# The last feed-forward stage of a four-layer kernel: order on VectorE, GpSimd and TensorE changed, layer-norm's scaling moved to ScalarE

## The reference, cut to what matters

```python
h = _layernorm(x) * (1 + cb) + sb
x_diff = h[:, None] - select_mean_diff[None, :, None, :]          # 8 experts
x_diff = x_diff / norm(x_diff)
score = (einsum('nds,bntd->bnts', select_weight, x_diff) ** 2).sum(-1)
gate = sigmoid(imp_slope * (score - imp_center))                  # per expert and token
sel_scale, sel_idx = gate.max(axis=1), gate.argmax(axis=1)
debias, bias, upd, dgn = rows of the tables at sel_idx
out = (1 - sel_scale) * h + sel_scale * (bias + dgn @ (upd^T (h - debias)))
x = x + gb * out
```

## Time and profile before

| | before |
|---|---|
| median of three runs | 1896.47 us |
| the profiled execution | 1898.01 us, its span 1895.8 us |
| mean granted clock of PE | 0.95 of full |
| busy share of PE, DVE, ACT, POOL | 88%, 71%, 44%, 53% |
| the chain that ended last | PE 56%, DVE 24%, issue 10% |
| the changed stage | from about 1752 us to the end |

### The profile page before, as it was taken

The page is one execution under the profiler, slowest core; times in us unless marked ns, Lnnn a source line. Parts: engine busy times, 40 slices in busy tenths (PEclk is TensorE's granted clock), DMA queues, the critical chain, the costliest instruction groups (busy, mean ns, idle before and its releaser), DMA issues.

```text
span 1895.8 us, 41681 instructions
## 1 busy us (share of the span) xinstructions
PE 1662.4 (88%) x14144; PEld 1200.9 (63%) x14144; DVE 1344.2 (71%) x3492; ACT 831.1 (44%) x1691; POOL 996.0 (53%) x1089
## 2 busy tenths in 40 slices
PE   5999997899996999999999879999867777999896
PEld 3666664799983555555555547777655555887443
DVE  5899996576654666767676657888745666887786
ACT  5556553222223566565656543333223333443442
POOL 2576676565553456564646354555543223666343
PEclk8999998899997999999999979999999888999988
DMA  7000000100026554546354300000001000000111
GB/s 263 18 18 17 12 18 9 35 12 9 11 48 142 115 104 101 111 88 125 76 122 93 72 7 15 12 8 8 23 27 44 14 14 20 12 14 17 33 45 53
DMA packets 70939, 94.13 MB, mean 50 GB/s; under 512 B 10461, under 2 KB 65165, under 8 KB 67597
## 3 DMA queue, kind: packets, MB, share of 16 engines
q1 hardware_dynamic: 70812, 92.41, 20.6%
HBM read 62.10 MB, written 29.49 MB: 48 GB/s over the span
## 4 chain that ended last, share of the span: by engine, by line
PE 56%; DVE 24%; issue 10%; ACT 5%; POOL 2%; DMA 1%; DVEq 1%; SPq 1%; ACTq 0%; POOLq 0%
PE PS L1173 19%; PE PS L2275 4%; PE PS L2365 3%; DVE negmax L2616 3%; PE PS L1362 3%; PE PS L573 2%; DVE l_acc L1782 2%; DVE st L521 2%; ACT pw L2518 2%; PE PS L2300 2%; PE PS L2220 2%; PE PS L2378 2%; DVE xn L542 1%; PE PS L843 1%; DVE rt_eq L1552 1%
## 5 line engine op out<-in xcount | busy, mean ns | idle before, releaser
L2616 DVE TENSOR_REDUCE negmax<-PS 128x2 f32<-128x512 f32 (+1 forms) x384 | 247.2, 686 | 166.3 <-PE PS L2275 160.6
L604 POOL TENSOR_TENSOR X<-X,y_sb 128x512 f32 (+1 forms) x128 | 163.2, 1275 | 113.7 <-DVE y_sb L599 108.7
L1173 PE MATMUL PS<-we_hi,h_parts 128*128 128x512 f32 x512 | 181.8, 411 | 16.5 <-DVE l_acc L1782 16.4
L2518 ACT ACTIVATE pw<-PS 128x512 f32<-128x512 f32 x256 | 139.2, 600 | 75.5 <-PE PS L2275 75.5
L583 ACT ACTIVATE hT<-PS,modT 128x256 f32<-128x256 f32 x256 | 130.4, 562 | 84.6 <-PE PS L573 83.1
L599 DVE TENSOR_TENSOR y_sb<-PS,ga_sb 128x512 f32<-128x512 f32 x96 | 66.1, 688 | 134.2 <-PE PS L2842 42.6
L1173 PE MATMUL PS<-l_h_parts,lut_hi 128*128 128x256 f32 (+1 forms) x704 | 132.7, 290 | 7.5 <-POOL l_h_parts L1327 7.5
L533 POOL TENSOR_TENSOR rs<-mv,eps 128x2 f32<-128x2 f32 x128 | 29.0, 226 | 187.8 <-DVE mv L526 187.6
L1173 PEld LDWEIGHTS PS<-we_hi,h_parts 128*128 128x128 f32 x512 | 98.2, 192 | 42.7 <-DVE l_acc L1782 15.0
L573 PE MATMUL PS<-ident,xn 128*128 128x128 f32 x512 | 85.3, 292 | 37.9 <-DVE xn L542 29.9
L1173 PEld LDWEIGHTS PS<-l_h_parts,lut_hi 128*128 128x128 f32 (+1 forms) x704 | 110.0, 191 | 10.2 <-issue 5.4
(11 more groups left out here) (328 smaller groups left out, 4585.1 us busy)
## 6 DMA issues: line engine op xcount, KB each, us to landing
ga_sb<-ga_dram SPq DMA_DIRECT2D x128, 128.0 KB, 2.9
qk_dram<-qk_parts SPq DMA_DIRECT2D x64, 192.0 KB, 2.8
KS<-qk_dram SPq DMA_DIRECT2D x32, 384.0 KB, 5.8
QS<-qk_dram SPq DMA_DIRECT2D x32, 384.0 KB, 9.0
qk_dram<-qk_parts SPq DMA_DIRECT2D x64, 128.0 KB, 2.8
wmod<-in_wmod SPq DMA_DIRECT2D x4, 1536.0 KB, 12.8
qk_dram<-qk_parts SPq DMA_DIRECT2D x64, 64.0 KB, 2.4
y_out<-X SPq DMA_DIRECT2D x16, 256.0 KB, 2.2
```

Of the source, the lines that this page charges most:

```text
L604: pool.tensor_tensor(xb(b), xb(b), y_sb[b.par][:, :, :], ALU.add).then_inc(s.x.sem, 1)
L1173: last_ = pe.matmul(out, x.bitcast(F32R), y.bitcast(F32R), start=start and n == 0, stop=stop and n == 2)
L2518: act.activation(to.rearrange("p a n -> p (a n)"), bank(4 + (2 * n + pr) % 3), ACT.Exp).then_inc(s.prob.sem, 1)
L2616: dve.tensor_reduce(to, src, AX.X, ALU.max, negate=True).then_inc(s.max.sem, 1)
```

## The change

In the last stage only:

- DVE no longer normalises batches 1 to 15; ACT does it with `ln_apply_scalar`, placed behind the exponential and ahead of `modulate`. Batch 0 is normalised on DVE by the stage before, as it was.
- POOL computes `shift` for these batches behind `ln_rstd`, and both now stand behind the gated residual.
- DVE's `choice` of i-1 stands directly behind `ratio`, ahead of `y1` of i-2, and the statistics of i+2 are last in the slot.
- PE's `out` of i-2 stands ahead of the transpose of i+1.
- The stage's signals get the two counts of `shift` per batch (`"qs": 2`).

```diff
-                       "tk": 7, ..., "y_ps": 1, "y1": 2},
+                       "tk": 7, ..., "y_ps": 1, "y1": 2, "qs": 2},
...
                 if (i - 1).ok:
                     rows_T(i - 1)
-                ahead(ln_transpose, pe, pl, i, 1)
                 if (i - 2).ok:
                     out(i - 2)
+                ahead(ln_transpose, pe, pl, i, 1)
                 if i.ok:
                     norms(i)
                     tokens(i)
...
                 if (i - 1).ok:
                     route_exp(act, pl, s, i - 1)
+                if (i + 1).ok and i.ok:
+                    ln_apply_scalar(act, pl, s, i + 1)
                 ahead(modulate, act, pl, i, 1)
...
-            def slot(i):
-                ahead(ln_apply, dve, pl, i, 1)
-                ahead(ln_stats, dve, pl, i, 2)
+
+
+            def slot(i):
                 if (i - 2).ok:
...
                 if (i - 1).ok:
                     ratio(i - 1)
+                    choice(i - 1)
                 if (i - 2).ok:
...
-                if (i - 1).ok:
-                    choice(i - 1)
+                ahead(ln_stats, dve, pl, i, 2)
...
             def slot(i):
-                ahead(ln_rstd, pool, pl, i, 2)
                 if (i - 2).ok:
                     gate_on_pool(pool, pl, s, i - 2, l3_y1[:, :, :], s.y1(i - 2))
+                ahead(ln_rstd, pool, pl, i, 2)
+                if i.reg is not None or 1 <= (i + 2).off < B:
+                    ln_shift(pool, pl, s, i + 2, 1)
```

More of the change, by code:

```diff
@@ L263, in build @@
             "L3_ffn": {"p_ps": 1, "hsq": 1, "sq": 1, "mx": 1, "ht": 1, "zr": 3, "z": 1, "zT_ps": 1,
-                       "tk": 7, "ed": 1, "e": 1, "g": 1, "oms": 1, "gT_ps": 1, "s_ps": 1, "zz": 1, "y_ps": 1, "y1": 2},
+                       "tk": 7, "ed": 1, "e": 1, "g": 1, "oms": 1, "gT_ps": 1, "s_ps": 1, "zz": 1, "y_ps": 1, "y1": 2, "qs": 2},
             "L2_attn": {"state_ps": 1, "state": 1},
```

## The result

The changed kernel takes 1906.98 us (median of 6 runs, 1903.03 to 1909.88), the kernel before on the same chip 1896.49 (6 runs, 1895.64 to 1898.99). The ratio is 1.0053, with a 95% interval of 1.0040 to 1.0067: slower, by 10.5 us. The forecast was slower as well, but by 4.1 us: 1900.6, with 1898 to 1906 as its own range and 1885 to 1908 as the range of all cases together. The measured time lies in the wide range and 1.0 us above the forecast's own.

What follows compares the result with a forecast made beforehand. It took a ring of waits through several engines as the limit, no engine being full. Terms 3.6 + 0.5 + 3.4 + 2.1 - 5.3 - 0.2 gave +4.1 us, 1900.6 against the median; own range 1898 to 1906, overall 1885 to 1908.

Steps and rivals of the forecast that it cites:

- the low clock: Slots 4 to 13: stretches with PE at 1.2 GHz cost 5.0 us after the change, against 3.5 before.
- Choice is freed of GpSimd: DVE in loop slots: choice meets an idle POOL, its two held operations take 0.17 us each, 1.64 us less per slot.
- The ring through ScalarE: Loop slots: reciprocal, exponential, ACT's xn, transpose, hT, L1980 and gates wait in turn, 8.0 us against 7.79; chance 0.44.
- the rival with 7.8: Loop slots: ScalarE's ring no longer than the old one, 7.8 us per slot, 1897.3 us in all; chance 0.27.
- GpSimd's order costs nothing: POOL, rstd and shift behind the residual: its two-slot ring takes 7.85 us per slot, with 0.15 us to spare.
- The first slots, +3.6: Slots 0 and 1: ACT's xn and the transpose now stand between mx and hT, 1.8 us each.
- The loop, +3.4: Nine slots from 4 to 13: 72.0 us plus 5.0 for the low clock, 77.0 against 73.60.
- Slots 13 to 15, +2.1: Two slots after the statistics had ended: the new ring still runs, 15.2 us against 13.05.
- The end, -5.3: Last two slots, 15 to 17: choice no longer waits behind y1, 4.4 us each, 8.8 against 14.10.
- The rival "PE takes over": Loop slots: xn slips in without holding hT, slots fall to PE's 6.4 to 6.6 us, 1885.5 in all; chance 0.19.
- The rival with POOL's ring: Loop slots: choice still meets POOL, 8.7 us per slot, +15 us, 1911.6 in all; chance 0.10.

Runs made afterwards that it cites:

- the old order: Changed kernel with statistics at the head of DVE's slot, and rstd and shift ahead of the residual on GpSimd, as before the change: ratio 1.0051.
- both moves of `xn` forward: Changed kernel with normalisation back at the head of DVE's slot, 1911.01 us; changed kernel with ScalarE's xn ahead of mx, 1911.42 us.
- the gaps filled: Changed kernel with two idle matmuls per slot between PE's out and transpose, from slot 0 on: 1899.59 us, ratio 0.9993.
- the fastest kernel above: Kernel before with choice ahead of y1, ht behind hsq on ACT, and statistics ahead of normalisation on DVE: 1880.33 us, ratio 0.9885.
- choice alone: Kernel before with one edit on DVE, choice of i-1 directly behind ratio and ahead of y1 of i-2: 1893.91 us, ratio 0.9971.
- old order: Changed kernel with PE's transpose of i+1 again ahead of out of i-2: 1932.43 us, ratio 1.0164.

## Why the prediction was right, and where it was short

The direction and the mechanism held, and so did the sign of each part down to slot 17. The size did not: +10.5 us in the medians against +4.1, which only the wide range holds. What was mis-sized is the low clock: it was counted in the loop alone, at 5.0 us, and put at nothing in the first slots and in slots 13 to 15.

- **Choice is freed of GpSimd.** Right: 0.17 to 0.18 us at L1552 and L1555, and DVE is bound no more (13.99 of 24 us).
- **The ring through ScalarE bounds the loop, 8.0 us.** Right. With the clock held at 1.00 the loop slot is (7.91 + 8.16)/2 = 8.04; the rival with 7.8 falls. In the slot above single terms came out longer and shorter: from the transpose's start to `hT` 1807.28 - 1806.44 = 0.84 us, where 0.70 had been taken, and from `hT` to L1980 1809.96 - 1807.28 = 2.68, where 2.54 had; the exponential to `xn` 0.23 for 0.30, and `xn` to the transpose 1.15 for 1.22. The hand-over of 0.05 had been read in a written-out slot; here it is 0.18.
- **GpSimd's order costs nothing.** Right for the change (ratio 1.0051 with the old order). Its margin was as small as said: both moves of `xn` forward that were tried met it.
- **The first slots, +3.6.** The step itself measured 3.9; 2.7 more came with the low clock behind PE's waits of 1.9 and 2.2 us (from L1948 to `zz` of slot 2 the granted clock was 0.79, against 0.91 before and 0.92 with the gaps filled). This term was mis-sized, because the low clock was put in for the loop alone. The 2.7 is no constant: with the same two waits the stretch took 23.6, 25.0 and 27.4 us in three profiles.
- **The loop, +3.4.** Measured +4.5. Nine slots at full clock are 72.2 us (forecast 72.0), the low clock 5.9 (forecast 5.0). The reason given for this term holds: PE was at 1.2 GHz for 17.4 us against 17.8 before, but these cost 5.9 us against 3.5, as more of PE's work now lies on the ring. The granted clocks of the two windows were 0.93 and 0.91 where the earlier trace rows had 1.00 and 0.79: the low stretches lay elsewhere, and their sum was the same.
- **Slots 13 to 15, +2.1.** Measured +3.8, of which 15.6 - 13.05 = 2.5 is the ring (filled kernel) and 1.3 the low clock of one slot.
- **The end, -5.3.** Measured -4.3. Slot 16 was as forecast (4.32), slot 17 took 5.46 instead of 4.4: POOL's residual of the batch before now meets `ratio` and the first step of `choice`. The 0.17 us of L2087 became 0.65 and the 0.17 of L2103 became 0.87, each ending with a POOL operation, while L2085 beside the first of these, with one input in PSUM, kept its 0.17:

```profile
1894.04 1.27 POOL L1820 TENSOR_TENSOR y_sb<-l_y,ga_sb 128x512 f32<-128x512 f32 x1 [5.05 <-DVE l_y L2130]
...
1894.49 0.17 DVE L2085 TENSOR_TENSOR l_rat<-l_rat,PS 128x16 f32<-128x16 f32 x1
...
1894.70 0.65 DVE L2087 TENSOR_TENSOR l_rat<-l_rat,l_sc 128x16 f32<-128x16 f32 x1
...
1895.39 1.28 POOL L604 TENSOR_TENSOR X<-X,y_sb 128x512 f32<-128x512 f32 x1
...
1895.83 0.87 DVE L2103 TENSOR_SCALAR l_ee<-l_ee 128x16 f32<-128x16 f32 x1 [0.28 <-ACT l_ee L1586]
```

Summed over the stage, filling the gap from slot 0 gives back 154.0 - 144.0 = 10.0 us in the profiles, and 1.0053 - 0.9993 = 0.6%, 11 us, in the runs; that kernel's stage stands 1.4 us above the stage of before. The forecast had 5.0 for the low clock. Of the 11.4 us that the stage lost, some 10.0 - 3.5 = 6.5 are thus the low clock beyond what it cost in the loop before, and 4.9 are the ring and the first steps less the gain at the end. What the stage of before lost to its own low stretches outside the loop was not measured, and no run here filled its gaps, so what that would give back is open.

The rival "PE takes over" was wrong as stated: `xn` did not slip in by itself. Its slots of 6.4 to 6.6 are what the fastest kernel above reached, 6.42, by other edits. The rival with POOL's ring did not decide either (in its working the residual ends 3.53 + 1.12 + 1.47 + 1.26 = 7.4 us after `zz`, not 7.5). The third ring, through `ht` and `y1`, was missed altogether; it did not change this forecast, as it is shorter than the first, but it made the forecast for choice alone wrong by some 10 us.

## What to carry to other kernels

When an operation is moved to an idle engine, what counts is what stands ahead of it there in program order: ScalarE was idle half the time, and the normalisation still lengthened every slot, since it came behind the one instruction that ends the critical chain. Before a chain is shortened, list each ring through its buffers (who overwrites what two batches later) as well as through its data: here three of nearly one length lay over each other, and the best version came from three reorderings within an engine, with nothing moved between engines. And a wait of one or two us on TensorE is dearer than its length if the clock falls behind it; whether it does is to be read from the granted clock, not from the length of the wait.

## What the runs showed of the hardware

- Two matmuls whose result nobody reads, 1.03 us per slot in a gap of 0.96 us, made the kernel faster: ratio 1.0053 became 1.0015, and 0.9993 with slots 0 and 1 filled. The granted clock went from 0.89 to 1.00 over the loop.
- The clock fell behind waits of TensorE of 1.9 us (slot 0) and in every second loop slot with waits of about 1 us, and with one wait of 2.3 us per slot (old order) in all but two of the loop slots. The kernel before had low stretches too, of which no run here shows the cause.
- The length of a wait alone does not tell whether the clock falls. With choice alone PE waited for `hsq` for 1.25 us or more in every loop slot, in one piece (1.43 in the row shown there), and the granted clock from 1787.7 to 1855.6 us was 1.00; in the change waits of about 1 us went with 0.89.
- What the low clock costs depends on how much of TensorE's work lies on the ring: about 17 us at 1.2 GHz in slots 4 to 13 cost 3.5 us before and 5.9 after.
- GpSimd's tensor operations hold not only VectorE's operations with two inputs in SBUF. `tensor_scalar` with one input and output in SBUF took 1.69 instead of 0.73 us (128x256, two of them, ending 0.15 us behind GpSimd's operation) and 0.87 instead of 0.17 (128x16, ending 0.03 behind it). The batch-norm statistics (0.74 us) and `tensor_tensor` with one of its inputs in PSUM (L2085 at 1894.49, 0.17) were not held.
